# The begin of a fused tokenizer and fast-weight kernel: first two weights loaded first and in three pieces, a product begun with the first piece, projection weights prepared between later steps

## The reference, cut to what matters

```python
# 64 images, 64 patches each, 768 numbers per patch; ATT = 192
q, k, v = (einsum('bnf,nfd->bnd', flat, W) + b for each of Wq, Wk, Wv)   # a weight of its own for each patch
attn = attention across the batch, patch by patch
att  = layernorm(attn) * ln_g + ln_b + flat @ p1_w + p1_b
h    = ((((att @ w0 + b0) @ w1 + b1) @ w2 + b2) @ w3 + b3) @ w4 + b4    # w0 192x768, w1..w3 768x768, w4 768x192
h    = softmax(h + att @ p2_w + p2_b)
h    = h + fast_weight_attention(layernorm(h))   # uses the k, q, v projections Wk, Wq, Wv and their modifiers
h    = h + ffn(layernorm(h))
```

## Time and profile before

| | |
|---|---|
| median of 3 runs | 1397.5 µs (1397.04 to 1405.56) |
| the profiled execution | 1401.61 µs, its span 1399.8 µs |
| TensorE busy | 1234.2 µs, 88% |
| VectorE busy | 816.8 µs, 58% |
| first stage, from its first matmul to the last pair | 75 to 434 µs |
| DMA share in that stage | 0.99, at about 373 GB/s |

### The profile page before, as it was taken

How to read it: one execution, slowest core, us unless ns; L and a number is a source line. 1 busy time by engine, 2 the same in 40 slices (tenths; PEclk the granted TensorE clock), 3 DMA queues, 4 the chain that set the end, 5 groups by cost and what they waited for, 6 DMA issues and landing times.

```text
span 1399.8 us, 45227 instructions
## 1 busy us (share of the span) xinstructions
PE 1234.2 (88%) x17572; PEld 1007.1 (72%) x17572; DVE 816.8 (58%) x2152; ACT 625.8 (45%) x1539; POOL 612.0 (44%) x721
## 2 busy tenths in 40 slices
PE   3879999999996569999999989999998999999874
PEld 3846666666664458788788878887887888888763
DVE  0173333333333246778768777876877777787652
ACT  0002222222222345666656656655665665666532
POOL 0000000000000364776677667567666766766621
PEclk9989999999997668999999999999999999999987
DMA  8859999999990001111111111111111111111110
GB/s 304 297 220 342 379 364 371 382 371 370 379 362 14 12 12 22 28 28 25 31 28 29 25 30 29 25 34 28 25 27 30 31 24 31 26 25 25 28 22 19
DMA packets 176410, 169.82 MB, mean 121 GB/s; under 512 B 118198, under 2 KB 146425, under 8 KB 175609
## 3 DMA queue, kind: packets, MB, share of 16 engines
q1 hardware_dynamic: 176234, 167.37, 37.0%
HBM read 154.72 MB, written 12.58 MB: 120 GB/s over the span
## 4 chain that ended last, share of the span: by engine, by line
PE 34%; POOL 32%; issue 17%; DVE 9%; DMA 3%; SPq 2%; ACT 2%; POOLq 0%; DVEq 0%; ACTq 0%
PE PS L435 29%; POOL region L1093 10%; POOL region L1074 4%; POOL region L1079 3%; POOL xr_lo L1098 2%; POOL region L1087 2%; POOL region L1050 2%; POOL region L1085 1%; POOL region L1054 1%; PE PS L504 1%; POOL region L1069 1%; POOL region L1057 1%; POOL region L1064 1%; PE PS L674 1%; DVE region L1447 1%
## 5 line engine op out<-in xcount | busy, mean ns | idle before, releaser
L435 PE MATMUL PS<-region 64*64 64x64 f32 (+5 forms) x5936 | 366.2, 288 | 46.5 <-DMA region<-in_w 23.2
L435 PEld LDWEIGHTS PS<-region 64*64 64x64 f32 (+3 forms) x5936 | 244.6, 140 | 145.1 <-issue 100.9
L1093 POOL TENSOR_TENSOR region<-region,powers 128x24 f32<-128x24 f32 x64 | 212.6, 3322 | 5.0
L1020 POOL TENSOR_TENSOR region<-region,powers 128x1 f32<-128x1 f32 x32 | 6.1, 192 | 417.5 <-DVE region L1201 417.5
L684 PE MATMUL PS<-region 64*64 64x64 f32 x4608 | 162.7, 226 | 2.3 <-ACT region L923 2.1
L684 PEld LDWEIGHTS PS<-region 64*64 64x64 f32 x4608 | 149.5, 141 | 21.0 <-issue 17.2
L1317 DVE TENSOR_REDUCE region<-region 128x12 f32<-128x768 f32 x96 | 91.0, 948 | 126.0 <-ACT region L895 126.0
L435 PE MATMUL PS<-cw_hi,xr_hi 128*128 128x512 f32 (+3 forms) x384 | 140.5, 366 | 10.0 <-POOL xr_lo L1098 10.0
L435 PE MATMUL PS<-cw_lo,xr_hi 128*128 128x512 f32 (+3 forms) x384 | 132.5, 345 | 0.0
L435 PE MATMUL PS<-cw_hi,xr_lo 128*128 128x512 f32 (+3 forms) x384 | 131.7, 343 | 0.0
L674 PE MATMUL PS<-region 64*64 64x64 f32 x3072 | 64.7, 232 | 63.8 <-DVE region L1336 31.4
(11 more groups left out here) (169 smaller groups left out, 2305.6 us busy)
## 6 DMA issues: line engine op xcount, KB each, us to landing
region<-in_Wq SPq DMA_DIRECT2D x32, 1152.0 KB, 5.9
region<-in_Wk SPq DMA_DIRECT2D x32, 1152.0 KB, 8.2
region<-in_Wv SPq DMA_DIRECT2D x32, 1152.0 KB, 7.8
region<-in_x SPq DMA_DIRECT2D x32, 384.0 KB, 6.8
region<-in_w SPq DMA_DIRECT2D x3, 2304.0 KB, 12.1
region<-h_scratch SPq DMA_DIRECT2D x64, 96.0 KB, 2.0
n_scratch<-region SPq DMA_DIRECT2D x256, 12.0 KB, 1.6
region<-i_scratch SPq DMA_DIRECT2D x256, 12.0 KB, 1.8
```

The costliest lines, as they stand in the source:

```text
L435: return nc.tensor.matmul(dst, lhsT, rhs, start=first, stop=last)
L1093: pool.tensor_tensor(rs[:, cols], rs_var[:, cols], root[:, cols], ALU.pow).then_inc(S["rs_ready"], 1)
```

## The change

The first two weights are loaded first, ahead of the small parameters, and each in three pieces of two row chunks, with a signal for each piece pair. w2 follows, then the small ones; w4 moves behind the first pair's loads and gets a signal of its own (`last_in`). The first product runs chunk by chunk in the outer loop and over all six output blocks inside, so it can begin with the first piece; it accumulates in all six blocks at once. VectorE's preparation of the projection weights moves into the first stage, in four parts: `centre_weights(0)` after its step 2, `split_weights(0)` after step 3, `centre_weights(1)` after step 4, `split_weights(1)` after step 5. Several signals are merged.

```diff
+            for g in range(3):
+                pair = slice(2 * g, 2 * g + 2)
+                sp.dma_start(bt[0][:, pair, :], d["w0T"][:, pair, :]).then_inc(S[f"first_in{g}"], 16)
+                sp.dma_start(chain_w[0][:, pair, :], d["w1"][:, pair, :]).then_inc(S[f"first_in{g}"], 16)
+            sp.dma_start(chain_w[1][:, :, :], d["w2"]).then_inc(S["chain_in1"], 16)
             for dst, src in small:
                 sp.dma_start(dst, src).then_inc(S["par_in"], 16)
-            sp.dma_start(bt[0][:, :, :], d["w0T"]).then_inc(S["chain_in0"], 16)
-            sp.dma_start(chain_w[0][:, :, :], d["w1"]).then_inc(S["chain_in0"], 16)
-            sp.dma_start(chain_w[1][:, :, :], d["w2"]).then_inc(S["chain_in1"], 16)
-            sp.dma_start(chain_w4[:, :, :], d["w4"]).then_inc(S["chain_in1"], 16)
...
             load_pair(Step(0, 0))
             load_biases(Step(0, 0))
+            sp.dma_start(chain_w4[:, :, :], d["w4"]).then_inc(S["last_in"], 16)
             sp.wait_ge(S["bt_copied"], 1)
...
+            for c_ in range(HC):
+                if c_ % 2 == 0:
+                    pe.wait_ge(S[f"first_in{c_ // 2}"], 32)
+                for i in range(HC):
+                    last = nc.tensor.matmul(chain_out(i), chain_w[0][:, c_, i * P:(i + 1) * P], bt[0][:, c_, :],
+                                            start=c_ == 0 and i % 2 == 0, stop=c_ == HC - 1, skip_group_check=True)
+            last.then_inc(S["bt_mm"], 1)
...
-            pipeline(dve, PAIRS, 2, step_b)
+            def step_b_and_weights(it, u):
+                step_b(it, u)
+                s = Step(it, u)
+                if s.known and 2 <= s.n < 6:
+                    (centre_weights, split_weights)[s.n % 2]((s.n - 2) // 2)
+
+            pipeline(dve, PAIRS, 4, step_b_and_weights)
```

More of the change, by code:

```diff
@@ L53 @@
 SIGNALS = """
- chain_in0 chain_in1 chain_in2 par_in cw_in bt_mm bt_copied bt_ready eff_mm eff_ready ffn_mm ffn_cols ffn_ready lr_exp
- lr_one lr_sig lr_ready beta_ready ones_set cw_scaled cw_sum cw_mean cw_centred cw_hi cw_ready wx_in0 wx_in1
+ first_in0 first_in1 first_in2 chain_in1 chain_in2 last_in par_in cw_in bt_mm bt_copied bt_ready eff_mm eff_ready ffn_mm ffn_cols ffn_ready lr_exp
+ lr_ready ones_set cw_step cw_ready wx_in0 wx_in1
  bias_in0 bias_in1 h_out0 h_out1 qkv_done qk_mm v_mm qk_copied v_copied tqk_mm qkT_ready scores_mm rmax_ready
@@ L435, in mm, with chain_out @@
                 return nc.tensor.matmul(dst, lhsT, rhs, start=first, stop=last)
[L438 to L443, removed]
+            def chain_out(i):
+                return PS[:, i // 2, (i % 2) * (ATT + 1):(i % 2 + 1) * (ATT + 1)]
+            for c_ in range(HC):
[5 more added lines that the diff above has]
+            last.then_inc(S["bt_mm"], 1)
+            for k in range(1, 3):
+                pe.wait_ge(S[("chain_in1", "chain_in2")[k - 1]], 16)
+                pe.wait_ge(S["bt_ready"], k)
                 w = chain_w[k % 2]
                 for i in range(HC):
-                    dst = PS[:, i // 2, (i % 2) * (ATT + 1):(i % 2 + 1) * (ATT + 1)]
                     for c_ in range(HC):
-                        last = mm(dst, w[:, c_, i * P:(i + 1) * P], bt[k % 2][:, c_, :], c_ == 0, c_ == HC - 1)
+                        last = mm(chain_out(i), w[:, c_, i * P:(i + 1) * P], bt[k % 2][:, c_, :], c_ == 0, c_ == HC - 1)
                 last.then_inc(S["bt_mm"], 1)
+            pe.wait_ge(S["last_in"], 16)
             pe.wait_ge(S["bt_ready"], 3)
@@ L1125, in _ @@
             dve.wait_ge(S["lr_exp"], 1)
[L1126 to L1129, removed]
+            dve.tensor_scalar(beta_h[:, :], lr[:, :], 1.0, None, ALU.add).then_inc(S["lr_ready"], 1)
+            dve.wait_ge(S["lr_ready"], 1)
+            dve.reciprocal(lrs[:, :], beta_h[:, :]).then_inc(S["lr_ready"], 1)
+            dve.wait_ge(S["lr_ready"], 2)
             dve.tensor_scalar(lr[:, :], lrs[:, :], 0.2, None, ALU.mult).then_inc(S["lr_ready"], 1)
-            dve.wait_ge(S["lr_ready"], 1)
-            dve.tensor_scalar(beta_h[:, :], lr[:, :], 1.0, None, ALU.add).then_inc(S["beta_ready"], 1)
+            dve.wait_ge(S["lr_ready"], 3)
+            dve.tensor_scalar(beta_h[:, :], lr[:, :], 1.0, None, ALU.add).then_inc(S["lr_ready"], 1)
             dve.tensor_scalar(half_g, lnv_g, 0.5, None, ALU.mult).then_inc(S["fold_ready"], 1)
@@ L1166, in _, with centre_weights @@
                 dve.tensor_scalar(wide[:, :], wide[:, :], ffn_mean[:, 2 + i:3 + i], None, ALU.subtract).then_inc(S["ffn_ready"], 1)
[L1170 to L1173, removed]
+            def centre_weights(k):
+                parts = (P, AUG)[k]
                 group = cw[0:parts, k, :].rearrange("p (g d) -> p g d", d=HD)
[L1175 to L1178, removed]
-                dve.tensor_tensor(group, group, cw_mean[0:parts, k, :].unsqueeze(2).to_broadcast([parts, GROUPS, HD]),
[L1180 to L1183, removed]
@@ new lines, in centre_weights @@
+                if k == 0:
+                    dve.wait_ge(S["cw_in"], 160)
+                    dve.tensor_scalar(cw[R2:AUG, 1, :], cw[R2:AUG, 1, :], 0.1, None, ALU.mult).then_inc(S["cw_step"], 1)
+                    dve.wait_ge(S["cw_step"], 1)
+                dve.tensor_reduce(cw_sum[0:parts, k, :], group, AX, ALU.add).then_inc(S["cw_step"], 1)
+                dve.wait_ge(S["cw_step"], 4 * k + 2)
+                dve.tensor_scalar(cw_mean[0:parts, k, :], cw_sum[0:parts, k, :], 1.0 / HD, None, ALU.mult).then_inc(S["cw_step"], 1)
@@ new lines, in centre_weights, with split_weights @@
+                dve.wait_ge(S["cw_step"], 4 * k + 3)
+                dve.tensor_tensor(group, group, cw_mean[0:parts, k, :].unsqueeze(2).to_broadcast([parts, GROUPS, HD]),
+                                  ALU.subtract).then_inc(S["cw_step"], 1)
+            def split_weights(k):
+                parts = (P, AUG)[k]
+                dve.wait_ge(S["cw_step"], 4 * k + 4)
+                dve.tensor_copy(cw_hi[0:parts, k, :], cw[0:parts, k, :]).then_inc(S["cw_step"], 1)
+                dve.wait_ge(S["cw_step"], 4 * k + 5)
@@ L1399, in inverse_norms @@
                 dve.wait_ge(S["n4"], j + 1)
-                dve.wait_ge(S["beta_ready"], 1)
+                dve.wait_ge(S["lr_ready"], 4)
                 dve.tensor_tensor(norm[:, 5, :], norm[:, 4, :], beta_h[:, 0:HEADS], ALU.mult).then_inc(S["rn_ready"], 1)
```

## The result

The changed kernel takes 1387.7 µs (median of 12 runs, 1377.2 to 1396.6) against 1399.9 for the kernel before (12 runs). The ratio is 0.991, with a 95% interval of 0.9885 to 0.9943: 12.2 µs less, and between 8 and 16 by the interval. Forecast were 12.6 µs less. The profiled execution has a span of 1384.4 µs.

The account below looks back on a forecast made before the run. The start was bound by a chain of waits through VectorE's wait for small loads, the stage by TensorE. Gains of 8.1 and 9.7 less 5.2 lost gave 12.6 µs, so 1384.9 µs, range 1377 to 1391.

Parts of the forecast that it names:

- step 1: First stage: with VectorE free of weight preparation, TensorE's step lasts 9.9 µs instead of 19.5, gaining 9.7.
- four stretched steps: First-stage steps carrying the four preparation parts: lateness over 3.7 µs stalls TensorE, 5.2 µs lost in all, no clock added.
- The begin: Program start: first product ends 18 µs earlier, but VectorE's wait for small loads leaves 8.1 µs gain at the stage's start.
- w3 had 3 µs to spare: Ahead of the third product: w3 lands at 42.2, before the handover at 45.5.
- The small loads: Twenty parameter loads behind w0, w1, w2: they take 7.8 µs and have all landed at 25.4.
- The rival by the transfer: Small loads cost by the transfer, landing at 29.2; gain at the start 8.8, total 1388.7 µs; chance 0.15.
- full rate: Rival: small loads take 4.0 µs and land at 19.2; gain at the start 16.9, total 1376.1 µs; chance 0.14.
- slack of 3.7 µs: Stretched first-stage steps: L1195 may start 3.7 µs after VectorE's last operation before TensorE stalls.
- VectorE's 2.2 idle µs: Smaller slack in a first-stage step; rival that all lateness beyond it counts gives 1393.6 µs, chance 0.08.
- the gap at 72.7: Before the first stage: after a 2.47 µs TensorE gap matmuls ran at full rate, so stalls got no clock cost.
- upper end that I gave for the stalls: First-stage stalls if everything over the 2.2 idle µs counts: 11.4 µs, summed elsewhere as 11.2.
- a second stage that changes by its clock: Sign of being wrong: the second stage was claimed to stay unchanged; no size given.

Follow-up runs that it names:

- Experiment 5: Changed kernel with w0 and w1 loaded first but whole, first product block by block; turn of step 32 at 424.5 µs against 424.0.
- experiment 3: Changed kernel with the chain's bias loaded ahead of w2 and VectorE's first copy ahead of its wait for the small loads; turn of step 32 at 425.6 µs.
- experiment 2: Changed kernel with the begin of the kernel before, so only the weight preparation is moved; ratio to before 0.9992 (0.9961 to 1.0023).
- experiment 4: Changed kernel with the weight preparation in ten parts behind steps 2 to 11; turn of step 32 6.5 µs earlier than in the changed kernel.
- 7: experiment 6 with w0 and w1 loaded whole and the first product block by block; turn of step 32 at 411.7 µs, 2.8 later.
- 1: Changed kernel with the projection weights prepared in one piece ahead of the first stage, as before; ratio to before 0.9952 (0.9928 to 0.9975).
- experiment 6: Changed kernel with early first copy, preparation in ten parts, and w3 and w4 ahead of the first pair's loads; 1372.3 µs, ratio to before 0.983.
- experiment 9: experiment 6 with TensorE's wait for the ffn weights moved behind the first stage; ratio to before 0.9855 (0.9796 to 0.9914).
- experiment 10: experiment 9 with the transfers into 64 and 49 partitions cut into six column pieces each and issued in turn; turn of step 32 3.3 µs earlier.

## Why the prediction was right

Each term of the sum against what the traces show:

| | forecast | measured |
|---|---|---|
| first matmul, end of first product | 5, 20 | 5.6, 19.5 |
| small loads landed | 25.4 | 25.25 |
| second product starts, and lasts | 29.0, 14.8 | 28.8, 14.3 |
| third product starts | 45.5 | 44.8 |
| stage starts; gain | 67.1; 8.1 | 66.5; 8.7 |
| clock at the stage's start | no cost | 1.7 lost |
| step 1 | 9.9 long, 9.7 gained | 9.6 long, 10.0 gained |
| four stretched steps | 5.2 lost | 6.2 lost |
| sum at the mark | 12.6 | 8.65 - 1.70 + 9.96 - 6.20 = 10.71 (by difference 10.70) |

**The begin.** The step that carried it was to follow VectorE's wait instead of TensorE's first matmul. Experiment 5 shows that 5 µs at the front are worth 0.5, and experiment 3 that the small loads were the link and w3 the next. My estimate that w3 had 3 µs to spare was somewhat high: it landed at 42.9 against my 42.2, and the third product started at 44.8, so 1.9 were left. In experiment 3 w3 landed at 44.0.

**The small loads.** Between the two prices, 4.0 by bytes and 9 by busy time, my 7.8 fitted: adding up the bytes of 2 µs windows of the changed kernel, 5.31 MB had moved at 15.2 and 6.95 at 23.1, so the small loads took 7.9 (an estimate from these windows). The choice was partly luck. Its reason, that loading of instructions had a part in the 9.2 busy µs, is not in the trace: all packets of the first 14 µs of before are those of the one queue of loads. The rival by the transfer (landing at 29.2) fell, and so did full rate (19.2). The issues were not all covered either. SP stood at one small issue for 4.1 µs and at another for 3.0, against 0.3 to 0.6 for most, while the DMA engines were busy.

**Step 1.** Right; the turn that I called pair 1's is pair 0's, turned in step 1; the rows and the arithmetic are those of step 1 all the same.

**The four stalls.** Without the clock they cost 4.7 (experiment 2) against 5.2, and ten parts below the slack cost nothing (experiment 4). So the slack of 3.7 µs, read from one step as the latest start that TensorE's turn allows, was right, and not VectorE's 2.2 idle µs. The mis-sized term is the clock, to which I gave nothing on the strength of the gap at 72.7 in the trace of before. After the same 2.5 µs of idling the clock fell at the stage's start in five of the nine traces that have it (the changed kernel and experiments 3, 4, 5, 7) and not in four (the kernel before and experiments 1, 2, 6); with the waits of step 3 (2.7 to 2.8 µs in two parts) it fell in four of five. It costs 1.6 to 1.7 µs each time. One trace in which a gap costs nothing does not show that it never does. The upper end that I gave for the stalls is 11.4 in one place and 11.2 in its own sum; 11.2 is right, and nothing hangs on it.

**The rest.** 12.2 µs in the medians against 10.7 at the mark: the second stage differs by up to 9 µs between traces of the same work, and each of the two clock falls, which an execution may have or not, moves the mark by 1.6 to 1.7. The interval of 8 to 16 µs cannot tell 10.7 from 12.6, so that 12.2 came out so near to 12.6 is luck; the terms of the sum are what was right. One of my signs of being wrong, a second stage that changes by its clock, does show between the two profiles (16 µs less at 0.50, 4.7 µs shorter). Over the twelve traces it comes and goes without regard to the change, so it was a bad sign to choose.

## What to carry to other kernels

When a first transfer is brought forward, follow the next engine's first wait in program order, and the transfer after that: here 18 µs at the front gave 8.7, because VectorE waited for parameters that had moved behind, and removing that wait alone gave nothing, since w3 stood next in line. Only with w3 brought forward too did the stage start earlier by another 8.5 µs. Work that is tucked into the steps of an engine off the critical path was free here while each part was shorter than the slack to the consumer's deadline, which is read from the last moment at which its operand is needed and not from the engine's idle time; ten small parts cost nothing where four larger ones cost 4.7 to 6.2 µs. And once transfers come near to pacing a stage, an earlier start can be lost again as a wait with low clock behind it: after experiment 6 a start 3.4 µs earlier brought the mark 4.9 later, in the one trace taken of each.

## What the runs showed of the hardware

- With an idle stretch of TensorE of only 2.5 µs the granted clock fell to 0.50 in five traces and stayed up in four, at the same place with the same work. Where it fell, 48 recorded matmuls took 7.6 to 7.7 µs instead of 6.04. After the idle start of the program (5.6 to 23.2 µs) the first product took 13.5 to 14.9 µs for the same 72 recorded instructions, 12.05 at full rate.
- While the projection weights were loaded, transfers into 64 and 49 partitions among them, the DMA engines were all busy (share 1.03) at 223 GB/s (experiment 9), where transfers into 128 had moved 435; with these two mixed in smaller pieces it was 285 (experiment 10). The cause is open, since the transfers into 128 partitions in the same stretch were slowed too.
- While the twenty small loads ran behind a full queue (16 to 20 µs of the changed kernel), the DMA engines had a share of 0.99 and moved 125 GB/s. So in this stretch it was the engines that were busy, and not the issuing that held them up.
